# The rest of k made on VectorE behind the tick's second row maximum, in a two-layer attention kernel

## What is computed

```python
# layer 0: cross-attention of x on the context, 16 heads of 8 features
xq, xkv = ada_ln(x, cond), ada_ln(ctx, cond)          # layer norm, scaled and shifted by cond
q = xq @ Wq + bq;  k, v = split(xkv @ Wkv + bkv)
x = x + softmax(q k^T / sqrt(8)) v @ Wp + bp
# layer 1: self-attention, cross-attention, MLP
q, k, v = split(modulate(ln(x)) @ W_qkv + b_qkv)
x = x + gate_a * (softmax(q k^T / sqrt(8)) v @ W_proj + b_proj)
q_c = ln(x) @ W_qc + b_qc;  k_c, v_c = split(ln(ctx) @ W_kvc + b_kvc)
x = x + softmax(q_c k_c^T / sqrt(8)) v_c @ W_cproj + b_cproj
x = x + gate_m * (gelu(modulate(ln(x)) @ W_mlp1 + b_mlp1) @ W_mlp2 + b_mlp2)
```

## Time and profile before

| | us |
|---|---|
| median of three runs | 348.33 |
| lowest and highest run | 347.09, 348.48 |
| the profiled execution | 346.47 |
| its span, first to last instruction | 344.6 |
| around the span | 1.87 |

### The profile page before, as it was taken

One profiled execution on the slowest core, in us unless ns is written; L12 is line 12 of the kernel. 1 busy time (PEld: TensorE's weight loads), 2 busy tenths in 40 slices (PEclk: granted clock), 3 DMA queues, 4 the chain that ended last, 5 costly groups with the idle time before them and its releaser, 6 DMA issues.

```text
span 344.6 us, 10197 instructions
## 1 busy us (share of the span) xinstructions
PE 283.7 (82%) x3827; PEld 181.3 (53%) x3827; DVE 247.7 (72%) x631; ACT 206.1 (60%) x324; POOL 130.7 (38%) x257
## 2 busy tenths in 40 slices
PE   0736549989899898998989889898897878879894
PEld 0413435656566565665655666555665555534342
DVE  6764795897887878778798787988879787613103
ACT  1324127676776756767676676676777667665540
POOL 8271942525225243153643646446352131301000
PEclk9975657999999999999999999999999999999998
DMA  6952311313131322323323233132231300000013
GB/s 193 306 140 57 91 49 50 93 49 90 55 95 49 94 68 77 80 64 95 83 64 96 56 87 95 52 93 66 80 95 52 95 3 4 5 0 2 1 30 91
DMA packets 31904, 25.39 MB, mean 74 GB/s; under 512 B 4552, under 2 KB 31600, under 8 KB 31856
## 3 DMA queue, kind: packets, MB, share of 16 engines
q1 hardware_dynamic: 30240, 23.49, 25.3%
q10 hardware_dynamic: 1616, 1.25, 1.2%
HBM read 4.41 MB, written 1.05 MB: 16 GB/s over the span
## 4 chain that ended last, share of the span: by engine, by line
PE 43%; DVE 26%; issue 15%; POOL 5%; ACT 4%; DMA 4%; SPq 1%; ACTq 1%; POOLq 0%; DVEq 0%
DVE normed L751 7%; PE attn_ps L426 7%; PE misc_ps L359 7%; PE keyed_ps L408 4%; DVE neg_max L770 4%; PE score_ps L473 4%; DVE stats L735 4%; PE keyed_ps L462 4%; DMA stack_q<-max_rows 4%; PE score_ps L384 3%; PE misc_ps L436 3%; PE misc_ps L367 3%; DVE rest L762 2%; PE misc_ps L343 2%; ACT parts L584 2%
## 5 line engine op out<-in xcount | busy, mean ns | idle before, releaser
L770 DVE TENSOR_REDUCE neg_max<-score_ps 128x8 f32<-128x1024 f32 x96 | 117.0, 1219 | 14.8 <-PE score_ps L384 14.8
L604 ACT ACTIVATE probs<-keyed_ps 128x1024 f32<-128x1024 f32 x96 | 98.3, 1024 | 12.7 <-PE keyed_ps L408 10.4
L426 PE MATMUL attn_ps<-probs,values 128*32 128x128 f32 x1536 | 62.0, 279 | 0.4 <-ACT probs L604 0.4
L408 PE MATMUL keyed_ps<-stack_q,stack_k 64*128 64x128 bf16 x768 | 38.6, 220 | 10.2 <-DMA stack_q<-max_rows 9.1
L426 PEld LDWEIGHTS attn_ps<-probs,values 128*32 128x32 f32 x1536 | 36.2, 109 | 19.9 <-issue 11.3
L904 POOL TENSOR_TENSOR rstd<-var_eps,minus_half 128x4 f32<-128x4 f32 x24 | 24.4, 1016 | 56.5 <-DVE var_eps L740 56.3
L384 PE MATMUL score_ps<-stack_k,stack_q 62*128 62x128 bf16 x768 | 38.8, 221 | 7.0 <-DVE neg_max L770 7.0
L911 POOL CAST max_parts<-neg_max 128x16 bf16<-128x16 f32 x48 | 10.2, 212 | 89.4 <-DVE neg_max L770 89.3
L570 ACT ACTIVATE normed_t<-misc_ps,mod 128x128 f32<-128x128 f32 x48 | 18.0, 456 | 33.1 <-PE misc_ps L349 24.2
L621 ACT ACTIVATE attn_t<-misc_ps,bcol 128x128 f32<-128x128 f32 x48 | 17.7, 368 | 32.3 <-PE misc_ps L441 30.8
L408 PEld LDWEIGHTS keyed_ps<-stack_q,stack_k 64*128 64x128 bf16 x768 | 21.9, 95 | 24.5 <-DMA stack_q<-max_rows 14.7
(11 more groups left out here) (94 smaller groups left out, 400.0 us busy)
## 6 DMA issues: line engine op xcount, KB each, us to landing
stack_q<-parts SPq DMA_DIRECT2D x72, 128.0 KB, 2.4
stack_k<-parts SPq DMA_DIRECT2D x72, 128.0 KB, 2.4
stack_q<-max_rows SPq DMA_DIRECT2D x96, 4.0 KB
xs<-in_x_dram SPq DMA_DIRECT2D x4, 256.0 KB, 6.3
cs<-in_ctx_dram SPq DMA_DIRECT2D x4, 256.0 KB, 6.3
out_dram<-xs SPq DMA_DIRECT2D x4, 256.0 KB, 2.3
w<-in_L_xcond_W_mlp_dram SPq DMA_DIRECT2D x2, 256.0 KB, 4.4
wmod<-in_L_xcond_W_mod_dram ACTq DMA_DIRECT2D x1, 384.0 KB, 4.7
```

The costliest lines, as they stand in the source:

```text
L408: mm = pe.matmul(keyed_ps[:, e, a * T:(a + 1) * T], stack_k[rows, g % STACKS, CP * c + a, cols], stack_q[rows, g % STACKS, CP * c + a, col ...
L426: mm = pe.matmul(attn_ps[at:at + QUAD, slot * T:(slot + 1) * T], values[:, u // PER % STACKS, u % PER, h, :], probs[:, n % 3, (CP * e + a) ...
L604: act.activation(probs[:, n % 3, :], keyed_ps[:, :, :].rearrange("t e n -> t (e n)"), ACT.Exp, scale=float(D) ** -0.5).then_inc(probs_read ...
L770: dve.tensor_reduce(neg_max[:, u % 2, :, CP * c:CP * (c + 1)], score_ps[:, :, :].rearrange("t e (a k) -> t e a k", k=T), AX.X, ALU.max, ne ...
```

## The change

`leave_rest(g3, 1)` of VectorE is moved from before the residual, the division and the second row maximum to behind that maximum. No instruction is added, removed or altered, and no other engine's program is touched. The order on VectorE is all that differs.

```diff
                 if norm:
                     norm_stats(*norm)
-                if g3 is not None:
-                    leave_rest(g3, 1)
                 if unit(tick - 2):
                     add_branch(tick - 2)
                 if unit(tick - 1):
                     divide(tick - 1)
                 if unit(tick + 2):
                     row_max(tick + 2, 1)
+                if g3 is not None:
+                    leave_rest(g3, 1)
                 if tick == FIRST:
                     copy_cond()
```

## The result

The changed kernel took 374.46 us (median of four runs, 371.91 to 376.19) against 348.40 us of the kernel before (347.09 to 348.85): ratio 1.075, 95% interval 1.068 to 1.082. It is 26.1 us slower. The profiled execution took 374.16 us, its span is 372.3 us, against 344.6 us before.

The account below looks back on a forecast made before the run. The prediction took TensorE's order to bound the kernel. To the profiled 346.47 us it added 20.0 us of stalls and 4.8 us of clock falls, 371.3, or 373.1 by the median; it forecast 372 us, range 364 to 379.

Parts of the forecast that it names:

- TensorE sets the pace in this tick, VectorE has room: Tick 13: TensorE's order bounds the tick; VectorE has 0.92 us idle ahead of its next maximum, its 0.45 us gain costed at 0.
- The stall: TensorE's gates or v wait for k's bank until the later rest: 2.04 us in nine ticks, 1.67 in tick 1, 20.0 together.
- Nobody absorbs the shift: Behind the stalled gates or v, the next maximum and tick 14's waits of 0.28 and 0.31 us move along without shrinking.
- GpSimd's split of the maxima is covered by 1 us: On GpSimd, the split behind k's rest ends near 131.9 us; TensorE's turn needs it at 132.95, so it costs nothing.
- The clock: TensorE's granted clock falls behind the 2.13 us pause in four of ten ticks, 1.2 us each: 4.8 us, bounds 0 to 16.
- The level: Whole kernel: 346.47 us profiled plus stall and clock falls gives 371.3, or 373.1 by the median; forecast 372.
- The rival without a fall: TensorE's stall alone, the clock staying up: 366.4 us profiled or 368.3 by the median; chance 0.32.

Follow-up runs that it names:

- e4: Changed kernel with another order of the three ring banks in ticks with k's projection, so gates and v don't take k's bank: 359.36 us, ratio 1.035.
- e7: Kernel before, with attend's second product with the values put ahead of gates and v in the ten ticks: 345.55 us, ratio 0.993.
- e8_half: Kernel before, with the move of k's rest made only in the six ticks 17 to 37: 363.20 us, ratio 1.045.
- e6_ring_pool: Changed kernel with e4's bank order, and on GpSimd the split of the maxima ahead of the split of k's rest: 355.24 us, ratio 1.021.
- e3_attend_first: Changed kernel, with attend's second product with the values ahead of gates and v in ticks with k's projection: 363.16 us, ratio 1.043.
- e1_rest_mid: Changed kernel, with k's rest put between the division and the second maximum instead of behind that maximum: 356.92 us, ratio 1.026.
- e2_filled: Changed kernel, with eleven dummy identity matmuls on TensorE in the pause of each of the ten ticks: 373.30 us, ratio 1.074.
- e5_filled_short: Changed kernel, with eight dummy identity matmuls on TensorE in each pause: 367.78 us, ratio 1.058.
- e9: e6_ring_pool, with the split of k's rest moved one tick later on GpSimd: 350.18 us, ratio 1.008.
- e10: Kernel before, with only e4's order of ring banks and the rest left in its place: 349.26 us, ratio 1.007.

## Why the prediction was right

The forecast was 372 us, in a range of 364 to 379; measured 374.46. Point by point, by its own steps:

- **TensorE sets the pace in this tick, VectorE has room.** Right. The 1.0 us of idle time taken from VectorE in each tick brought nothing; it waits 2.64 us later on.
- **The stall.** Rest 1.13 us behind the maximum, 2.04 us a tick, 2.13 us of standing still: measured 1.13, 2.03 and 2.14. Tick 1 was put at 1.67 us and measured 1.5. The sum of 20.0 us comes out of the changed trace as 20.1, the falls taken off, and the filled kernel gives 20.0 by the medians, 367.8 against 347.8.
- **Nobody absorbs the shift.** Right. The waits in the following ticks moved along. One tick, 13, got 0.27 us longer than the sum has; VectorE's residual stood idle 1.52 us there, put down to GpSimd's bias, a wait that I had not weighed. It is small, and I didn't follow it.
- **GpSimd's split of the maxima is covered by 1 us.** Right for the changed kernel in tick 13 (split done at 142.35, turn at 143.42 us). In tick 17, which has no gates, the cover was 0.64 us (165.96 against 166.60), less than the prediction has. And e4 shows what it costs without the cover: 11.9 us of waiting. The prediction named this cover but not the third one, the gated addition in the self-attention layer.
- **The clock.** Four falls predicted, four seen; that the count agreed is luck, since it was picked between none and ten. The price of a fall was sized at 1.2 us and measured at 1.4 to 1.6, so 6.0 and not 4.8 us: the measured price is a quarter above the term. What was undersized is attend. It was priced by the 0.80 us at 55.74, but that instruction ran across the clock's return at 56.10; wholly at the lower clock it took the 1.08 us shown above, so it adds 0.4 us a fall and not 0.15. The 0.85 us for v was right: in tick 21 it took 1.97 us until attend, in tick 17 1.09. Tick 1 had a fall too, although its pause was the shortest, 1.51 us.
- **The level.** By the profiled execution the sum was 371.3, and it took 374.16: 1.2 us from the price of a fall, 0.3 from tick 13, and 1.5 us from the start, where the rest of q in tick 0 began at 58.08 and not at 56.57, ahead of any tick that the change touches. That belongs to the single execution and not to the change: over the twelve traces this rest began between 56.3 and 58.6 us, and in the four latest, the changed kernel's among them, one early instruction of VectorE (line 682 in the changed kernel) took 3.35 us, where it took 1.61 in the kernel before. By the median it was 373.1 against 374.46.
- **The rival without a fall.** It stood at 366.4 us by the profiled execution and 368.3 by the median. The kernel with the pause filled took 367.5 and 367.8, so the stall was right, and the clock is what the rival lacked: pauses of 1.43 us (e4) to 2.14 us (tick 29), and the one of 2.38 us, were followed by falls. The Trainium skill's page "TensorE: Matmul & The Clock Gate" (section "Why this matters for your kernels") warns of longer pauses only; this trace doesn't agree with reading it as a promise for shorter ones.

## What to carry to other kernels

Before moving a step back on an engine that has idle time, look for the resource it frees, here a PSUM bank in a ring, and for who takes that resource next: the cost is how far the step moves past that moment, not how busy its engine is. A step moved late hides further costs under its first wait; here the order of the banks and two steps in GpSimd's queue had to be changed before the move was nearly free, and it never became a gain. Where an engine waits a little for such a bank, work already at hand put ahead of the wait gives the time back at once, as e7 did with 2.2 us.

## What was not expected of the hardware

The granted clock fell behind pauses of TensorE shorter than the 2.38 us in the earlier trace rows, and the length of the pause doesn't settle it. The table has the attention part of each trace, from tick 1 on, and its pauses of TensorE of over 0.9 us:

| kernel | pauses | their length, us | with a fall |
|---|---|---|---|
| changed | 10 | 1.51 to 2.39 | 4 |
| e8_half | 6 | 2.13 to 2.14 | 3 |
| e6_ring_pool | 4 | 1.79 to 1.80 | 3 |
| e3_attend_first | 10 | 0.93 to 1.84 | 1 |
| e4_ring | 6 | 1.43 to 1.44 | 5 |
| e1_rest_mid | 9 | 1.00 to 1.27 | 0 |
| e2_filled, e5_filled_short | none | | 0 |

The longest pause, 2.39 us in the changed kernel, had no fall, and e4's falls, behind its shortest ones, lasted up to 6.8 us. A long pause isn't needed either: in e9 the clock fell at 244.76 us with no pause over 0.59 us near it, and at the end of the attention part it fell in e1, e3, e7 and e10 behind a wait of 0.68 us that the kernel before has too, without a fall. What decides it was not found.

Dummy matmuls in the pauses kept the clock at 1.00 in all ten ticks of both kernels, where 4 of 10 pauses had a fall without them. They cost nothing that the trace shows in the nine ticks where they ended in time.
